# Layer 2 of a four-layer kernel: two recurrences and two attention halves of a batch merged into one loop of 16 steps

## What is computed

```python
G = sigmoid(einsum('ntd,hed->nhet', X, w_G) + b_G)        # gates, 8 heads, E = 4
A = 1.0 - minimum(G.sum(axis=1), 1.0)                     # decays
gK = einsum('nhet,nhtd->netd', G, K); gV = einsum('nhet,nhtd->netd', G, V)
# t is cut as (L = 32, tc): a scan along tc in each of E x L chains
nK = _pscan(A, gK, iK); nV = _pscan(A, gV, iV)
uk = recK[:, :, idx]; uv = recV[:, :, idx]                # a window of 32 states for each token
scores = einsum('nhtd,netld->nhtel', Q, uk) / sqrt(64)
probs = softmax(scores over the 4 x 32 states)
out = einsum('nhtel,netld->nthd', probs, uv) @ w_O        # times silu(RWKV feed-forward)
```

## Time and profile before

| | |
|---|---|
| time, three runs | 817.3, 817.35, 825.04 us; median 817.35 us |
| the profiled execution | 819.91 us, its span on the core 818.1 us |
| busy | TensorE 702.2 us (86%), VectorE 420.7 us (51%), ScalarE 378.1 us (46%), GpSimd 183.5 us (22%) |
| mean granted TensorE clock | 0.925 of full speed |
| layer 2, batch 0 / batch 1 | from 324.7 to 481.3 us / from 577.2 to 721.8 us of the span |

### The profile page before, as it was taken

How to read it: one execution, slowest core, us unless ns; L and a number is a source line. 1 busy time by engine, 2 the same in 40 slices (tenths; PEclk the granted TensorE clock), 3 DMA queues, 4 the chain that set the end, 5 groups by cost and what they waited for, 6 DMA issues and landing times.

```text
span 818.1 us, 12659 instructions
## 1 busy us (share of the span) xinstructions
PE 702.2 (86%) x4303; PEld 456.0 (56%) x4303; DVE 420.7 (51%) x950; ACT 378.1 (46%) x864; POOL 183.5 (22%) x189
## 2 busy tenths in 40 slices
PE   4769797989699899975896799899897996899896
PEld 1558352479676567744673564455665773554453
DVE  1732662356235534546633855756538324856754
ACT  5401556463266462563345834344457355743332
POOL 2000028004446101753310620000107311600000
PEclk9857688999799999997998999999999998999999
DMA  8700003036545221100000000000000000000000
GB/s 315 266 0 1 0 11 119 13 91 189 164 127 149 68 71 45 44 17 1 2 1 1 1 1 0 14 1 0 14 1 2 2 2 0 2 0 1 14 1 13
DMA packets 24237, 36.05 MB, mean 44 GB/s; under 512 B 2856, under 2 KB 14992, under 8 KB 23664
## 3 DMA queue, kind: packets, MB, share of 16 engines
q1 hardware_dynamic: 21200, 28.04, 10.5%
q0 software_dynamic: 2976, 7.21, 3.1%
HBM read 26.00 MB, written 9.18 MB: 43 GB/s over the span
## 4 chain that ended last, share of the span: by engine, by line
PE 66%; DVE 12%; ACT 9%; issue 6%; POOL 5%; DMA 1%; DVEq 0%; ACTq 0%; SPq 0%; POOLq 0%
PE bank L546 62%; ACT arena L1116 5%; POOL arena L2397 2%; POOL slots_in L2331 2%; ACT L1116 2%; POOL arena L2405 1%; DVE bank L2114 1%; DVE arena L2117 1%; PE bank L891 1%; ACT rs L1116 1%; PE bank L982 1%; PE bank L841 1%; DMA x<-in_x 1%; DVE arena L2246 1%; ACT sq L1116 0%
## 5 line engine op out<-in xcount | busy, mean ns | idle before, releaser
L1116 ACT ACTIVATE arena<-bank 128x512 f32<-128x512 f32 (+7 forms) x238 | 134.1, 567 | 208.8 <-PE bank L546 96.6
L546 PE MATMUL bank<-arena 128*64 128x128 f32 (+7 forms) x1088 | 140.1, 338 | 14.7 <-DVE arena L1727 10.9
L546 PE MATMUL bank<-arena,w 128*128 128x512 f32 (+2 forms) x272 | 130.0, 600 | 12.3 <-ACT arena L1116 8.9
L546 PEld LDWEIGHTS bank<-arena 128*64 128x64 f32 (+4 forms) x1088 | 100.5, 176 | 56.1 <-issue 20.5
L1116 ACT ACTIVATE arena<-bank,arena 128x128 f32<-128x128 f32 (+1 forms) x244 | 87.6, 386 | 93.3 <-PE bank L546 50.5
L546 PE MATMUL bank<-arena,work 128*128 128x128 f32 x624 | 92.7, 285 | 5.9 <-DVE arena L2004 4.0
L546 PE MATMUL bank<-xn_b,w 128*128 128x512 f32 (+1 forms) x192 | 91.4, 600 | 3.1 <-DVE arena L2246 3.1
L546 PEld LDWEIGHTS bank<-arena,work 128*128 128x128 f32 x624 | 81.5, 197 | 17.1 <-issue 15.3
L546 PEld LDWEIGHTS bank<-arena,w 128*128 128x128 f32 (+1 forms) x272 | 48.0, 199 | 53.2 <-issue 32.4
L2331 POOL DMA_INDIRECT slots_in<-arena x32 | 33.4, 1044 | 121.1 <-ACT arena L1116 112.1
L546 PEld LDWEIGHTS bank<-xn_b,w 128*128 128x128 f32 (+1 forms) x192 | 35.1, 191 | 41.7 <-issue 29.3
(11 more groups left out here) (211 smaller groups left out, 953.4 us busy)
## 6 DMA issues: line engine op xcount, KB each, us to landing
work<-in_ew SPq DMA_DIRECT2D x46, 256.0 KB, 3.1
slots_in<-work SPq DMA_DIRECT2D x2, 1472.0 KB, 18.7
arena<-slots_in SPq DMA_DIRECT2D x10, 256.0 KB, 3.7
slots_out<-arena POOLq DMA_DIRECT2D x10, 256.0 KB, 2.9
w_ew<-in_ew SPq DMA_DIRECT2D x1, 2048.0 KB, 12.8
w<-in_p SPq DMA_DIRECT2D x1, 1840.5 KB, 10.2
...
```

Of the source, the lines that this page charges most:

```text
L546: return nc.tensor.matmul(o, lhsT, rhs, start=start, stop=stop, skip_group_check=True)
L1116: return nc.scalar.activation(o, i, f, bias=bias, scale=scale, **kw)
```

## The change

`layer2()` replaces the four calls. After `recurrence(0)` comes one loop with n from 0 to 19: n is `place(n)` = (g, m), so that steps 0 to 7 are the attention of half 0 and steps 8 to 15 that of half 1, and only one drain of four steps is left. `recurrence(1)` is cut into ten pieces, and `RECUR` says how many of them each step of the loop runs. On TensorE: decays 0 with spread in step 0; products 0 and decays 1 in step 1; products 1 and states 0 in step 2; decays 2 in step 3; products 2, values 0, states 1 in step 4; decays 3 in step 5; products 3, values 1, states 2 in step 6; values 2, states 3 and both queries in step 7; values 3 in step 8. T1 moves to steps 9 to 13. `finish(2, 0)` moves from before recurrence 1 to step 12, the norm of the next layer from recurrence 1 to steps 13 to 15, `entry3(0)` to steps 15 to 17, and most of `route3(0)` behind the loop. `gates()` makes both halves at once, in the place of `gates(0)`; so `gtm` and `gsum` have room for two halves. The gates spread over the chunks are copied out of PSUM to `spread_g` at once. A `pv` bank now stays in `growing` until its second `value`.

The core of the diff:

```diff
-ATT_SIDE = [{4: 1, 5: 1, 6: 2, 7: 2, 8: 1}, {3: 1, 4: 1, 6: 1, 7: 2, 8: 2, 9: 3}]
+RECUR = {0: 1, 1: 2, 2: 1, 3: 1, 4: 1, 5: 1, 6: 1, 7: 1, 8: 1}
...
-LATER = {5: "T1", 6: "T1", 7: "T1", 8: "T1", 9: "T1"}
+LATER = {9: "T1", 10: "T1", 11: "T1", 12: "T1", 13: "T1"}
...
-                def gates(g):
-                    ring = "slow" if g else "quick"
-                    pe.wait_ge(*at("xn", 2, g))
-                    o = fresh(ring, "gt", g)
-                    for c in range(C):
-                        i = mm(o[:, c * 32:(c + 1) * 32], xn[2][:, gs(g)][:, cs(c)], W2["wg"])
-                    i.then_inc(*step("gt", g))
-
-                def layer2_rec(g):
+                def gates():
+                    for g in range(G):
+                        pe.wait_ge(*at("xn", 2, g))
+                        o = fresh("quick", "gt", g)
+                        for c in range(C):
...
                         decays(c)
                         if c == 0:
                             spread()
+                        yield
                         products(c)
-                        if c == 1:
-                            queries(0)
+                        if c == 1 and g == 0:
+                            queries(0, 0)
                         if c >= 2:
                             values_of(c - 2)
                         if c >= 1:
                             states_of(c - 1)
-                    queries(1)
-                    if g == 1:
-                        norm(3, 0)
+                        yield
+                    if g == 0:
+                        queries(0, 1)
                     values_of(C - 2)
                     states_of(C - 1)
-                    if g == 1:
-                        variance(3, 0)
+                    yield
                     values_of(C - 1)
-                    growing.discard((now[1], "g2", g))
-
-                def layer2_att(g):
-
-                    pe.wait_ge(*at("xk", g))
-                    mm(fresh("quick", "r2", g)[:], W2["wr"], xr[:]).then_inc(*step("r2", g))
-                    mm(fresh("quick", "k2", g)[:], W2["wk"], xk[:]).then_inc(*step("k2", g))
+                    yield
...
                             pv_bank[0] = fresh("slow", "pv", g, m // 2)
-                            if m == 0:
-                                pe.wait_ge(*at("vt_s", g, C - 1))
+                            pe.wait_ge(*at("vt_s", g, m // 2))
...
+                        if m % 2:
+                            growing.discard((now[1], "pv", g, m // 2))
...
+                    for _ in recurrence(0):
+                        pass
+                    coming, entry = recurrence(1), entry3(0)
+                    for n in range(2 * MB + 4):
+                        if n in (0, MB):
+                            mixers(n // MB)
+                        if n in (1, MB + 1):
+                            o = fresh("slow", "v2", n // MB)
+                            pe.wait_ge(*at("kr", n // MB))
+                            mm(o[:], W2["wv"], kr[:]).then_inc(*step("v2", n // MB))
+                        if n < 2 * MB:
+                            score(n)
+                        if 2 <= n < 2 * MB + 2:
+                            turned(n - 2)
+                        if 4 <= n:
+                            value(n - 4)
+                        if n in (MB + 1, 2 * MB + 1):
+                            project(n // MB - 1, 0)
+                        if n in (MB + 3, 2 * MB + 3):
+                            project(n // MB - 1, 1)
+                        for _ in range(RECUR.get(n, 0)):
+                            next(coming)
+                        if n == MB - 1:
+                            queries(1, 0)
+                            queries(1, 1)
+                        if now[1] == 0 and n in LATER:
+                            advance(LATER[n])
+                        if n == MB + 5:
+                            norm(3, 0)
+                        if n == MB + 6:
+                            variance(3, 0)
+                        if n >= MB + 7:
                             next(entry, None)
-                        if now[1] == 0 and g == 0 and m in LATER:
-                            advance(LATER[m])
-                        if m < MB:
-                            score(m)
-                        if 2 <= m < MB + 2:
-                            turned(m - 2)
-                        if 4 <= m:
-                            value(m - 4)
-                        if m == MB + 1:
-                            project(0)
-                    project(1)
...
+                    coming, ahead = recurrence(1), entry3(0)
+                    for n in range(2 * MB + 4):
+                        if n in (0, MB):
+                            mixers(n // MB)
+                        if n in (4, MB + 4):
+                            after(("of", n // MB), *([("hz", 0)] if n > MB else []))
+                            fn(tz[:], of[:], ACT.Tanh, scale=0.25).then_inc(*step("tz", 2, n // MB))
+                        if 2 <= n < 2 * MB + 2:
+                            turned(n - 2)
+                        if n < 2 * MB:
+                            probs(n)
+                        if n >= 5 and n % 2 == 1:
+                            out_rows(*divmod((n - 5) // 2, MB // 2))
+                        for _ in range(RECUR.get(n, 0)):
+                            next(coming)
+                        if n == MB - 1:
+                            queries(1, 0)
+                            queries(1, 1)
+                        if now[1] == 0 and n in LATER:
+                            advance(LATER[n])
+                        if n == MB + 5:
+                            square(3, 0)
+                        if n == MB + 6:
+                            rsqrt(3, 0)
+                        if n >= MB + 8:
                             next(ahead, None)
...
+                def gates():
+
+                    for g in range(G):
+                        after(("gt", g))
+                        v.tensor_tensor(gtm[:, g].rearrange("p c h e -> p c (h e)"),
+                                        psum("gt", g)[:, 0:C * 32].rearrange("p (c k) -> p c k", k=32),
+                                        w_bg[:].rearrange("p (a k) -> p a k", a=1).to_broadcast([P, C, 32]),
+                                        ALU.add).then_inc(*step("gtz", g))
+                        reached[("gt", g, "read")] = reached[("gtz", g)]
+                    yield
+                    after(("gtx",))
                     v.tensor_scalar(gtm[:], gtm[:], 1.0, None, ALU.add).then_inc(*step())
-                    yield
                     after()
                     v.reciprocal(gtm[:], gtm[:]).then_inc(*step())
-                    yield
-                    after()
-                    v.tensor_reduce(gsum[:], gtm[:].rearrange("p c h e -> p c e h"), AX.X, ALU.add).then_inc(
-                        *step("gsum", g))
+                    after()
+                    for g in range(G):
+                        v.tensor_reduce(gsum[:, g], gtm[:, g].rearrange("p c h e -> p c e h"), AX.X, ALU.add).then_inc(
+                            *step("gsum", g))
...
+                        if c == 0:
+                            after(("g2", g))
+                            v.tensor_copy(spread_g[:], psum("g2", g)[:, 0:2 * C * 16]).then_inc(*step("g2", g, "read"))
+                        yield
...
+                    coming, side, routed = recurrence(1), [mixed(0), mixed(1)], route3(0)
+                    for n in range(2 * MB + 4):
+                        if n == MB + 4:
+                            finish(2, 0, hz[:], 0.25)
+                        if n < 2 * MB:
+                            maxima(n)
+                        if n in (2, 3, 5, MB + 2, MB + 3, MB + 5):
+                            next(side[n // MB], None)
+                        if 1 <= n < 2 * MB + 1:
+                            sums(n - 1)
+                        if 2 <= n < 2 * MB + 2:
+                            newer(n - 2)
+                        for _ in range(RECUR.get(n, 0)):
+                            next(coming)
+                        if n == MB - 2:
+                            for _ in shift(1):
+                                pass
+                        if now[1] == 0 and n in LATER:
+                            advance(LATER[n])
+                        if n == MB + 7:
+                            dve.wait_ge(ready["three"], 32)
+                            norm(3, 0)
+                        if n in (MB + 8, MB + 9):
+                            next(routed)
+                    for _ in routed:
+                        pass
+                    finish(2, 1, hz[:], 0.25)
...
+                    coming = recurrence(1)
+                    for n in range(2 * MB + 4):
+                        if n < 2 * MB:
+                            g, m = place(n)
+                            pool.wait_ge(*at("rc2", g, m))
```

(7 more changed lines are left out.)

323 lines of the change are left out of this document (133 added, 190 removed).

## The result

The changed kernel took 841.57 us (median of 4 runs, 841.00 to 842.72) and the kernel before 821.19 us on the same chip: a ratio of 1.024, 95% interval 1.016 to 1.032. It is 2.4% slower; the forecast was 807 us, 1.3% faster. The profiled execution took 842.72 us with a span of 840.9, 22.8 us more than the 818.1 before.

A forecast was written before the change was run, and what follows sets the result against it. TensorE is busiest, its gaps in layer 2 filled by a chain of waits through four engines. Batch 1 -7.3, batch 0 -8.2, gates +5.0 make -10.5 us: median from 817.35 to 807 us, range 798 to 812 (0.50).

The forecast's parts named there:

- four waits behind `out_rows`: TensorE waits before decays 3, values 2, projections 0 and 1: 2.2 us each, 8.8 in all in batch 1.
- projection 1: In batch 0, TensorE's wait for the projection in step 11 grows from 2.2 to 5.1 us, through VectorE's `weighed` and `summed`.
- Score 2: In the merged loop, this score waits for the exponentials of score 1, whose bank pair it takes: 2.2 us.
- rt3: TensorE's first product of layer 3 waits 4.1 us for the norm of layer 3.
- the rest .83 and .74: Old waits that remain: 0.8 us for the last values of recurrence 0 and 0.74 before the last projection.
- rival of ScalarE as the bound: ScalarE's recurrence evictions delay TensorE 1.3 us in each of 16 steps, 21 us: 828 us, slower; chance 0.10.
- The gates: Making both halves in "N0" and "N1" gives back 2 x 2.5 = 5.0 us; 2.0 if VectorE's part is hidden.
- removed waits of 4.74 and 1.62 us: Waits at the end of recurrence 1, for layer 3's norm and VectorE's token shift.
- the waits that come instead: TensorE's uncovered waits in the new order of layer 2: 18.0 us in batch 1, 24.6 us in batch 0.
- the clock: Busy time TensorE loses to a low clock in layer 2: 3.3 us in batch 0, between 0 and 6.7.
- sign of being wrong: Forecast is wrong if waits on ScalarE are absent or in every step, or the loop's clock is below 0.9.
- the clock takes it back: Waits of 2 us in every second step lower the clock, costing 10 us in all: 817 us, no change; chance 0.23.

The follow-up runs named there:

- ScalarE's order: Changed kernel with `out_rows` placed ahead of the four exponentials of its step on ScalarE; ratio 1.007 to the kernel before.
- second profile of the changed kernel: The changed kernel run again unedited on another chip; 841.57 us, ratio 1.028 to the kernel before.
- GpSimd's order alone: Changed kernel with GpSimd taking the recurrence's pieces first in each step of the loop; ratio 1.000 to the kernel before.
- The fillers: Changed kernel with 15 unread identity products ahead of states 0, ratio 1.016 to the kernel before; with 11 more ahead of layer 3's first routing product, 1.020.
- the kernel with both orders: Changed kernel with GpSimd taking recurrence pieces first and ScalarE copying value rows before the exponentials; 804.46 us, ratio .980 to the kernel before.
- the gates split: Changed kernel with both queue orders changed, plus half 1's gates made inside recurrence 0; 799.24 us, ratio .974 to the kernel before.

## Why the prediction was wrong, step by step

**Right.** The four waits behind `out_rows` stand where they were placed: 2.19, 2.19, 2.19 and 2.20 us against 2.2 each, in batch 0 projection 1 waits 4.21 against 5.1. Score 2 waits 2.04 against 2.2, rt3 3.53 against 4.1 (2.00 in batch 0), the rest .83 and .74. ScalarE's order shows the cause of the four. The rival of ScalarE as the bound had the sign of the result but not its way: in batch 1 TensorE waits for ScalarE only at the places that the forecast lists and .61 us at one score. The gates cost 4.0 us, between the lower bound of 2.0 and the 5.0 of the sum; the 2.0 in layer 3 stand in every profile in which both gates are made at once, those ahead of batch 0 are less sure (in the second profile of the changed kernel the first decays begin at 324.19 us, though the wait of 1.23 us is there). The removed waits of 4.74 and 1.62 us are gone.

**The step that failed first: the waits that come instead.** The list of what is not covered, 18.0 us, was made by placing TensorE, ScalarE and VectorE; GpSimd's queue was not walked, and the `mix` was taken as there when its growth was. In step 1 it stands behind `prob(1)`, which needs a reciprocal that VectorE makes a step later, and behind `older_half(0)`. Missing were 4.68 and .98 us, and for the bank of v2, which VectorE reads late, 1.72: 7.4 us in batch 1, against 6.5 us that its idle time (24.5 us) lies over the forecast. Batch 0's idle time is 7.8 us over. GpSimd's order alone shows this step's weight: layer 2 is back at the lengths of the kernel before. What T1 and the moved `finish` and norm add to batch 0 was not tested by itself.

**The step that failed most: the clock.** The forecast had nothing for it in batch 1 and 3.3 us in batch 0; it was 8.6 and 14.6 (8.9 and 10.8 in the second profile). The forecast's own sign of being wrong, a clock below 0.9 in the loop, came true in batch 0. The rival "the clock takes it back" priced it at 10 us in two batches, in addition to the forecast, and named its mechanism; the measured 19.9 us above the forecast is twice that. It was sized from a single stretch and set against a count of waits that left out the longest one. The fillers show that the wait before states 0 drags the clock, and in the kernel with both orders, in which the waits of batch 1 sum to 14.9 us, only .9 us there are lost to it. So the two failed steps are not independent: GpSimd's order alone, which ends two of the missed waits, also gave back 5.2 of the 8.6 us in batch 1.

The sum closes: -10.5 us forecast, +6.5 + 7.8 for waits, +8.6 + 11.3 for the clock, -1.0 for the gates, +22.7 of the measured 22.8.

**What the forecast's idea was worth.** With the two queues put in order, layer 2 takes 144.7 and 135.2 us up to the end of the last projection, as the forecast counts, below the 148.4 and 137.3 that it gave to the change as it is: it counted the four waits at 2.2 us, and they are .76. The merged loop is a gain of 2.0%, and of 2.6% with the gates split, made a loss of 2.4% by the order in which two engines take their pieces of a step.
